# A copy and a transpose moved forward, and ACT's loop without its hint, in the attention stage of a fused attention and expert kernel

## The reference

```python
x = x + tanh(g_xattn[0]) * attention(layernorm(x), ctx_512, ctx_512)   # softmax(q k / sqrt(32)) v, 4 query heads a kv head
x = x + tanh(g_ffn[0]) * moe(layernorm(x), w_cls, bias, w_gate_up, w_down)
# moe: scores = softmax(x @ w_cls.T); top 8 of scores + bias; weights normalised, times 1.5
#      y_e = (silu(x_e @ gate) * (x_e @ up)) @ down for the 32 routed experts, summed by weight
```

## Time and profile before

| | |
|---|---|
| time, median of 3 runs | 2402.77 us (2398.74 to 2402.88) |
| profiled execution | 2402.77 us, span 2401.0 us |
| PE, PEld, DVE, ACT, POOL busy | 88%, 52%, 63%, 54%, 36% of the span |
| 60 to 917 us (attention): busy of 857 | PE 712.21, DVE 718.49, ACT 614.31, POOL 395.14 |
| 917 to 2401 us (experts): busy of 1484 | PE 1378.53, DVE 762.47, ACT 667.73, POOL 453.63 |
| mean granted TensorE clock | 0.961 |

### The profile page before, as it was taken

The page is one execution under the profiler, slowest core; times in us unless marked ns, Lnnn a source line. Parts: engine busy times, 40 slices in busy tenths (PEclk is TensorE's granted clock), DMA queues, the critical chain, the costliest instruction groups (busy, mean ns, idle before and its releaser), DMA issues. The chain is left out here.

```text
span 2401.0 us, 45917 instructions
## 1 busy us (share of the span) xinstructions
PE 2115.4 (88%) x15296; PEld 1253.2 (52%) x15297; DVE 1509.3 (63%) x2730; ACT 1302.1 (54%) x1894; POOL 867.2 (36%) x893
## 2 busy tenths in 40 slices
PE   4998888988889825899999989899989899989976
PEld 2554545555555413446556564554655676554454
DVE  4789999999989662235545574553554775553373
ACT  3787777777777621235435463543453654443364
POOL 3113455555545563113224251421242433221152
PEclk9999999999999967999999999999999999989998
DMA  4354433544334344357967867685595997766563
GB/s 119 89 166 118 128 113 117 154 121 126 116 110 121 92 121 142 101 137 176 248 162 167 235 177 208 173 239 139 117 267 132 239 251 197 212 150 195 144 158 92
DMA packets 456150, 376.26 MB, mean 157 GB/s; under 512 B 109654, under 2 KB 377046, under 8 KB 456080
## 3 DMA queue, kind: packets, MB, share of 16 engines
q1 hardware_dynamic: 411024, 303.27, 44.3%
q0 software_dynamic: 45056, 72.09, 14.2%
HBM read 310.94 MB, written 101.06 MB: 172 GB/s over the span
## 5 line engine op out<-in xcount | busy, mean ns | idle before, releaser
L1386 PE MATMUL psum<-xgt,wgu 128*128 128x256 f16 (+3 forms) x6144 | 859.3, 303 | 31.9 <-DVE wgu L1057 21.9
L1386 PEld LDWEIGHTS psum<-xgt,wgu 128*128 128x128 f16 x6144 | 550.7, 99 | 339.2 <-DVE wgu L1057 23.9
L556 POOL TENSOR_TENSOR spare<-spare 128x1 f32<-128x1 f32 x264 | 133.7, 506 | 1068.0 <-PE psum L1395 457.3
L1395 PE MATMUL psum<-wdn,apair 128*128 128x512 f16 x1944 | 458.4, 387 | 48.5 <-ACT ys L839 39.8
L922 DVE TENSOR_REDUCE mx<-psum 128x2 f32<-128x512 f32 x512 | 328.9, 686 | 76.6 <-PE psum L1232 66.8
L1133 DVE COPY xgt<-psum 128x1024 f16<-128x1024 f16 x256 | 168.1, 687 | 301.4 <-PE psum L1371 279.1
L839 ACT ACTIVATE ys<-psum,slots 128x512 f32<-128x512 f32 x256 | 162.7, 689 | 317.2 <-PE psum L1395 314.3
L1143 DVE SCALAR_TENSOR_TENSOR a<-psum,sg 128x512 f32<-128x512 f32 x128 | 88.2, 689 | 387.7 <-PE psum L1386 387.7
L1395 PEld LDWEIGHTS psum<-wdn,apair 128*128 128x128 f16 x1944 | 186.6, 99 | 251.1 <-issue 48.0
L1057 DVE SCALAR_TENSOR_TENSOR wgu<-wraw,wgu 128x1024 f16<-128x1024 f32 x256 | 311.5, 1218 | 0.0
L594 POOL DMA_INDIRECT lists<-entry,dest x256 | 281.0, 1098 | 83.7 <-issue 82.1
(11 more groups left out here) (131 smaller groups left out, 1997.4 us busy)
## 6 DMA issues: line engine op xcount, KB each, us to landing
wraw<-in_L_ffn_w_gate_up_dram SPq DMA_DIRECT2D x256, 512.0 KB, 5.6
wraw<-in_L_ffn_w_down_dram SPq DMA_DIRECT2D x128, 512.0 KB, 6.6
x<-in_x_dram SPq DMA_DIRECT2D x16, 1024.0 KB
qs<-qh SPq DMA_DIRECT2D x256, 64.0 KB
xr<-in_x_dram SPq DMA_DIRECT2D x16, 1024.0 KB
out_dram<-x SPq DMA_DIRECT2D x16, 1024.0 KB
pairs<-xs SPq DMA_DIRECT2D x16, 1024.0 KB, 4.1
qs<-ql SPq DMA_DIRECT2D x128, 64.0 KB
```

The source lines that it names most:

```text
L1386: mm = pe.matmul(ps_gu[:, s, h, 0:nt * P], w[:, a, k, :], xgt[:, c, k, 0:nt * P], start=(k == 0 and (a, c) == (0, 0)), stop=(k == KB - 1 a ...
L1395: mm = pe.matmul(psum[:, Y_BANK[i] + n2, :], apair[:, o, k, c * P:(c + 1) * P], w[:, a, k, :], start=(k == 0 and (a, o) == (0, 0)), stop=( ...
```

## The change

On ACT, in round 7 the copies of Q3 (`q_stack(b + 2, 3)`) come ahead of `take_heads`; in rounds 1 and 2 `norm_q` comes behind `m_rows` and `x_stack`; and ACT's attention loop is built without the back-edge hint. On PE, the X1 transposes come right behind K0's, ahead of the first value products of round 0, and no longer at the round's end. The order of fills in the banks is the same.

```diff
@@ ACT, step
                     if on(b, 0):
                         exps(b, kv, 1)
+                    if kv == 7 and on(b, 2):
+                        q_stack(b + 2, 3)
                     if kv < 2 and on(b, -1):
                         take_heads(b - 1, kv + KV - 2)
                     if kv >= 2 and on(b, 0):
                         take_heads(b, kv - 2)
-                    if kv == 7 and on(b, 2):
-                        q_stack(b + 2, 3)
-                    if kv in (1, 2) and on(b, 2):
-                        norm_q(b + 2, kv - 1)
                     if kv == 1 and on(b, 0):
                         m_rows(b, 1)
                     if kv < 3 and on(b, -2):
                         x_stack(b - 2, kv + 1)
+                    if kv in (1, 2) and on(b, 2):
+                        norm_q(b + 2, kv - 1)
@@
-            loops(act, step, mybir.EngineType.Activation)
+            loops(act, step)
@@ PE, step
                     if kv in Q_SLOT and on(b, 2):
                         q_transpose(b + 2, Q_SLOT[kv])
+                    if kv == 0 and on(b, -2):
+                        x_transpose(b - 2, 1)
                     valued(kv, 0)
@@
-                    if kv in (0, 1, 2) and on(b, -2):
+                    if kv in (1, 2) and on(b, -2):
                         x_transpose(b - 2, kv + 1)
```

## The result

The changed kernel takes 2426.68 us (2424.33 to 2429.65, 4 runs), the kernel before 2401.24 us on the same chip: ratio 1.0107, 95% interval 1.009 to 1.0125. It is slower, by 25.4 us. The profiled execution took 2429.58 us (span 2427.9), 26.9 us of span more than before. The forecast was 2413.9 with a range to 2421: the sign was right, more than half of the loss was missed.

What follows compares the result with a forecast made beforehand. It took three nearly full engines (PE, DVE, ACT), passing work through PSUM pairs two deep, to bound the attention stage. 2402.8 + 10.3 + 0.8 + 0 = 2413.9 us; range 2403 to 2421, the forecast's own 2409 to 2419.

Steps and rivals of the forecast that it cites:

- Part 1: ACT, round 7, Q3 copies ahead of the head copy: exponentials of round 0 0.50 us later, cost alone 0.
- Part 2: PE, X1 behind K0: PE idles about 1.9 us, attention steps slip, 10.3 us in sum, bounds 5 and 27.
- 8.75 us chain: Attention step, from x_stack(0)'s old start to the (1,0) score products' new start: 8.75 us, making even steps 0.71 longer.
- The lower bound of the forecast: Attention loop: if ACT's waits end 0.2 to 0.3 us earlier, inner steps cost 0 and 5 us remain.
- Part 3: ACT, rounds 1 and 2, norm_q behind m_rows and x_stack: Q0's wait stays, now for xq; cost 0.8 us.
- The 0.8 us: ACT, x_stack(3) right behind the X3 transposes, no longer covered by norm_q: 0.07 us in each of 12 steps.
- Part 4: ACT's attention loop without the back-edge hint: loop bodies stay resident, cost 0, at most 7.5 us.
- rival A: ACT's taken back edges: the hint was needed, four edges at 1.87 us more, 2421 us; chance 0.16.
- bound of 1.87: ACT's four taken back edges: upper bound for a code-load stall at each, taken from PE's stall at the loop's exit.
- B: Attention steps: nothing measurable, DVE's lateness and ACT's idle time absorb the inner steps, 2404 us (2399 to 2407); chance 0.22.
- C: Attention steps: faster, Q0's 0.86 us wait goes in 11 steps, 9.5 us, and X1 is free, 2393; chance 0.10.

Runs made afterwards that it cites:

- e5: Kernel before with only ACT's swap in round 7, Q3 copies ahead of the head copy: 2400.93 us, ratio 1.0005.
- e2: Changed kernel with ACT's back-edge hint kept, so only the order changes: 2411.93 us, ratio 1.0045.
- e7: Kernel before with the round 7 swap and X1 moved behind K0, hint kept, norm_q in its old place: 2416.7 us, ratio 1.0069.
- e8: Changed kernel with hint kept, plus 24 identity matmuls, results unused, between K0 and X1: 2410.01 us, ratio 1.0039.
- e6: Kernel before with only norm_q moved behind m_rows and x_stack: 2400.77 us, ratio 1.0.
- e3: Kernel before with only X1 moved right behind K0, hint kept: 2404.0 us, ratio 1.0018.
- e15: Changed kernel, no hint, with the head of ACT's loop placed at the start of a code block: 15.7 us slower than the kernel before.
- e14: Changed kernel, no hint, plus identity matmuls ahead of X1 (64 in the loop's odd steps, 24 elsewhere): four executions, 2421.84 to 2432.83 us.
- e13: Changed kernel measured once more on a chip like the first: it repeats the result, with odd steps of 55.02 us.
- e1: Kernel before with only ACT's back-edge hint taken away: 2403.28 us, ratio 1.0009.
- e10: Changed kernel, no hint, ACT's loop head at the start of a code block, on a slower chip: 2484.64 us, ratio 1.0039.
- e4: Changed kernel with X1 back in its old place, no hint, swap and norm_q as changed: 2404.53 us, ratio 1.0014.
- e16: Kernel before with X1 moved behind K0 and no hint on ACT: 20.9 us slower than the kernel before.
- e9: Changed kernel, no hint, plus 64 or 24 identity matmuls ahead of X1, on a slower chip: 2490.2 us, ratio 1.0068.

## Why the prediction was wrong

**Part 1, right.** 0 alone (e5), and the exponentials came 0.5 us later. What the prediction didn't ask was what this half microsecond does to the clock once X1 waits for it.

**Part 2, the mechanism right, its sum right by offsetting errors.** Forecast for the orders alone: 10.3 and 0.8, or 11.1 us; e2 measured 12.0 (7.4 to 13.9 by the interval), e7 without part 3 16.3. That the sum came near e2 is luck. X1 was to start 3.82 behind X0 and started at 3.81; the idle of "about 1.9" was 1.74. The terms were off:
- Even steps 0.31, not 0.71. The mis-sized term of the 8.75 us chain is the 2.61 from scores_t to the end of the value products: between 462.29 and 464.72 it was 2.43, and the pitches behind it were 0.06 shorter together; scores_t had come 0.04 sooner. That is 0.28 of the 0.40. The lower bound of the forecast was worked out wrongly: waits that end 0.2 to 0.3 us earlier leave 0.4 of the 0.71, not 0, and 0.31 is what remained.
- Odd steps 1.44 with the hint, not 0.27, and all of it half clock: with the clock held (e8) they lose nothing. The prediction had no term for TensorE's clock, though it put an idle of 1.9 us into each step. That is the first step that failed: the prediction took the pitches of step 8, at clock 1.00, for what lies behind the idle.
- Step 2 2.03 (forecast 2.35), steps 14 and 15 together 0.61 (2.9), steps 3 and 13 1.65 (0.4). Step 13's 1.64 is half clock too, and X1 isn't needed for it: PE stands 1.63 us for "issue" at the loop's exit, and the clock is 0.50 from about 723.4 to 726.8. e6, with X1 in its old place, has the same (51.18), and e3, with X1 moved, has not (49.92).

**Part 3, right where it mattered.** Q0's wait stayed and is now for xq. TensorE's waits of the changed kernel in 240 to 700 us, which answer to the earlier trace rows:

```profile
PE psum L1282 <- ACT xt L734: 25.3, 9, 4.3
PE psum L1245 <- ACT prob L750: 19.8, 29, 1.2
PE psum L1209 <- ACT xq L686: 9.0, 9, 1.0
PE psum L1232 <- DVE mx L922: 4.6, 18, 0.4
```

The 0.8 us were not to be seen (e6: 0.3 us, interval around 0, even steps 0.05 longer). The last row is the other thing foretold: the waits for DVE's maxima, 17.1 us in 45 times before, are down to 4.6 in 18, since PE comes late itself.

**Part 4, the step that failed.** "Loop bodies stay resident; I take 0" rested on the earlier trace rows. Those rows showed hinted loops, and the unhinted ones of GpSimd and SyncE, and rival A itself says that ACT's body is larger than theirs. Without the hint q14 moves 5 packets (40 KB) and ACT stands 2.2 to 2.9 us at each taken edge. Even the bound of 1.87 from the earlier trace rows was too low. By the Trainium skill ("Runtime: NRT & Kernel Launch", Instruction fetch mechanics) a taken branch to a page outside of the two-page window waits for its load, and I set this aside as not borne out; the rows of the changed kernel bear it out. e15 fits it too: a body that starts on a page's first instruction may lie in two pages where it lay in three. That is an argument only; no run varied the body's length, and how the hint keeps the loads away (hinted, no packet moved at all in 343 to 695) isn't shown either.

**Rival A was the case, with two prices missing.** Its mechanism is there at its four edges. It was priced at 1.87 an edge, 7.5 in all; the gap alone costs 2.36 a step (e14), and then come about 1.9 (e13 less e14) to 2.4 us (X1 to the value products in step 9) of half clock behind the idle that the gap stretches from 1.74 to 4.09. The parts don't add up, and the prediction added them: in e1 the gap has the value products of round 0 as cover, and part 2 takes just this cover away.

**B and C.** B fell: DVE's lateness absorbs the delay in odd steps, as it said, but not in even ones, and it too left out the clock. C fell as foretold: Q0's wait stayed at 1.0.

**What stays open.** Why 1.74 us of idle is followed by full clock in nearly all even steps and by half clock in the odd ones of e2; step 10 of the changed kernel (half clock) and steps 5 and 7 of e15 (full clock) show that it isn't the parity alone. Nor does the length of the idle decide it, as the list at the end shows. And why one execution of e14 lost in the expert stage what it had gained.

## What to carry to other kernels

Ask of a reordered wait not only how long the engine stands, but at what clock it comes back: here a 4 us idle of TensorE cost up to 2.4 us more behind its end, and two edits that cost 3 and 4 us alone cost 21 together because one took the other's cover. Half clock comes in some steps and not in others behind the same idle, so compare step by step before you charge it to an edit. Resident code under a hinted loop is no evidence for the unhinted one. Keep the hint on the loops of full engines or place the loop's head, and look at the packet counts of the instruction queues after any edit to a loop.

## What the runs showed of the hardware

- A taken back edge without hint stops ACT for 2.2 to 2.9 us and VectorE for 3.3 to 3.4, with 5 packets (ACT) or 6 (VectorE) of 8 KB a time. With its head at the start of a code block, ACT's unhinted loop shows no gap at its taken edges and 31 packets in all, and one stand of 1.2 (e10) or 1.4 us (e15) at its entry.
- The granted clock behind an idle stretch of TensorE in the attention stage: 1.00 behind 0.40 (e8) and 0.44 us (e14), where matmuls whose result nobody reads fill the rest. Behind 1.14 to 1.88 us it was at either level: 0.50 behind 1.14 (e3, step 3, a wait for DVE), 1.36 (e1, step 3), 1.75 and 1.80 (e1, steps 5 and 11) and 1.88 (e4, step 5), 1.00 behind 1.25 (e3, X1), 1.69 and 1.45 (e1, steps 7 and 9) and 1.76 (e4, step 9), both behind 1.74 (e2). Behind 3.9 to 4.3 us (changed kernel, e13, e16) it was 0.50 in every step behind a taken edge, for 3 to 5 us of PE's work. The kernel before has such a stretch too, in step 14 (786.2 to 789.6 us, behind 1.61).
- In one execution with such padding (e14) PE stood 6.9 us more for "issue" in the next stage, with 4 more packets on q8; in another of the same kernel (e9) it had no more packets.
